# Edge biases summed in 64 buckets of one tile and 16 columns instead of 32 buckets of two tiles and 32 columns, in one kernel of two graph transformer layers

## The reference, cut to what matters

```python
x = x + _L0_gnn_ref(xn, ..., edge_index, edge_attr_16, Wq, bq, Wk, bk, Wv, bv, Wo, bo, We, be, 32) \
      + _L0_mix_ref(xn[None], Wq, Wk, Wv, Wo, bo, proj)      # random feature attention
x = x + _L0_ffn_ref(...)                                     # gated delta rule, 4 experts
x = x + _L1_gnn_ref(xn, edge_attr_64, edge_index, ...) + _L1_mix_ref(xn, ...)
x = x + _L1_ffn_ref(...)
```

## Time and profile before

| | |
|---|---|
| median of 3 runs | 3136.3 us (3127.96 to 3140.72) |
| the profiled execution | 3123.57 us, span 3120.5 us |
| busy, share of the span | PE 91%, DVE 54%, POOL 48%, ACT 40% |
| mean granted TensorE clock | 0.963 of full speed |
| sort on DVE | 39.4 to 137.2 us from the span's start |
| random feature stage after the sort | 180.4 to 646 us |
| bias stage, first to last add | 655.4 to 819.4 us |

### The profile page before, as it was taken

The page is one execution under the profiler, slowest core; times in us unless marked ns, Lnnn a source line. Parts: engine busy times, 40 slices in busy tenths (PEclk is TensorE's granted clock), DMA queues, the critical chain, the costliest instruction groups (busy, mean ns, idle before and its releaser), DMA issues.

```text
span 3120.5 us, 46071 instructions
## 1 busy us (share of the span) xinstructions
PE 2838.8 (91%) x16072; PEld 1657.1 (53%) x16072; DVE 1674.4 (54%) x3673; ACT 1245.0 (40%) x2883; POOL 1503.9 (48%) x1469
## 2 busy tenths in 40 slices
PE   6999999988899989968999998999989999999828
PEld 3433466667677644446777765444534444444324
DVE  7633355568544452256777743442258989521361
ACT  3312432269322222255666542221057888431201
POOL 0565756568754438643333203554667777200004
PEclk9999999999999999979999998999999999999859
DMA  5400001120111134524445555211167777400504
GB/s 178 144 20 5 7 23 42 55 73 18 28 48 48 46 115 164 199 81 133 132 130 147 149 157 159 84 54 50 31 193 234 227 224 216 138 15 12 189 0 136
DMA packets 275656, 320.31 MB, mean 103 GB/s; under 512 B 155759, under 2 KB 193521, under 8 KB 275428
## 3 DMA queue, kind: packets, MB, share of 16 engines
q1 hardware_dynamic: 219540, 182.05, 19.2%
q0 software_dynamic: 51680, 134.08, 14.0%
q10 hardware_dynamic: 4208, 1.25, 0.2%
HBM read 214.70 MB, written 104.60 MB: 102 GB/s over the span
## 4 chain that ended last, share of the span: by engine, by line
PE 69%; POOL 8%; issue 7%; ACT 6%; DVE 6%; DMA 2%; SPq 1%; ACTq 0%; PEld 0%; DVEq 0%; POOLq 0%; PEldq 0%
POOL conv_src L2757 7%; PE bank L1534 5%; PE bank L714 4%; PE bank L2420 4%; PE bank L1312 4%; PE bank L2984 4%; PE bank L2977 4%; PE bank L445 3%; PE bank L737 2%; PE bank L768 2%; PE bank L1123 2%; PE bank L2400 2%; PE bank L1322 2%; PE bank L864 2%; PE bank L2177 2%
## 5 line engine op out<-in xcount | busy, mean ns | idle before, releaser
L2757 POOL DMA_INDIRECT conv_src<-xn_rows,keep x286 | 291.1, 1018 | 110.3 <-issue 91.6
L297 POOL DMA_INDIRECT sorted_bias<-perf_rec,place x256 | 259.3, 1013 | 146.3 <-PE bank L714 91.9
L2862 DVE TENSOR_TENSOR conv_msg<-bank,conv_src 128x1024 f32<-128x1024 f32 x143 | 175.1, 1224 | 52.8 <-PE bank L2777 40.5
L672 POOL DMA_INDIRECT sorted_edge<-rec,place x128 | 126.8, 991 | 128.7 <-PE bank L1373 69.1
L1953 POOL TENSOR_TENSOR delta_dec<-delta_dec,rates_of 128x512 f32<-128x512 f32 x64 | 67.4, 1053 | 227.4 <-ACT delta_dec L2012 227.4
L1123 PE MATMUL bank<-bias_prod,bias_hot 128*128 128x256 f32 x640 | 148.3, 387 | 25.3 <-ACT bias_hot L1076 13.1
L2777 PE MATMUL bank<-conv_we,conv_eT 64*128 64x512 f32 x572 | 164.2, 651 | 0.2 <-ACT conv_eT L2834 0.2
L1107 POOL TENSOR_TENSOR bias_prod<-bias_col,bias_rec 128x512 f32<-128x512 f32 x128 | 147.3, 1181 | 16.5 <-PE bank L1123 15.7
L1123 PEld LDWEIGHTS bank<-bias_prod,bias_hot 128*128 128x128 f32 x640 | 120.1, 192 | 53.9 <-issue 28.2
L2786 PE MATMUL bank<-conv_msg,conv_hot 128*128 128x512 f32 x288 | 143.5, 621 | 0.0
L2219 DVE TENSOR_TENSOR delta_BA<-bank,delta_dec 128x512 f32<-128x512 f32 x128 | 82.1, 683 | 97.3 <-issue 59.8
(11 more groups left out here) (510 smaller groups left out, 6996.6 us busy)
## 6 DMA issues: line engine op xcount, KB each, us to landing
keep<-slot_qkv SPq DMA_DIRECT2D x32, 512.0 KB, 4.8
delta_kv<-slot_qkv SPq DMA_DIRECT2D x32, 512.0 KB, 3.9
sorted_edge<-sort_pad SPq DMA_DIRECT2D x8, 1440.0 KB, 7.0
keep<-sorted_edge SPq DMA_DIRECT2D x18, 640.0 KB, 4.5
slot_out<-delta_o SPq DMA_DIRECT2D x64, 128.0 KB, 2.7
conv_src<-xn_rows,keep POOLq DMA_INDIRECT x286, 3.8
X<-in_x SPq DMA_DIRECT2D x4, 1024.0 KB, 11.3
sorted_bias<-perf_rec,place POOLq DMA_INDIRECT x256
```

The costliest lines, as they stand in the source:

```text
L297: POOL.indirect_dma_start(out=sorted_bias, out_offset=bass.IndirectOffsetOnAxis(ap=place[:, 0, c:c + 1], axis=0), in_=rec0[:, c, :], in_of ...
L672: POOL.indirect_dma_start(out=sorted_edge, out_offset=bass.IndirectOffsetOnAxis(ap=place_[:, c - skip:c - skip + 1], axis=0), in_=rec1[:, ...
L2757: POOL.indirect_dma_start(out=src[:, n % 4, j, :], out_offset=None, in_=xn_rows, in_offset=bass.IndirectOffsetOnAxis(ap=rec[:, g % 3, k + ...
L2862: DVE.tensor_tensor(msg[:, q, :, :], pairs[1 + q][:, :, :], src[:, n % 4, :, :], ALU.add).then_inc(*raw.up())
```

## The change

- `PARTS = 4` in place of `HALVES = 2`: 64 buckets of 16 columns. `TB = 1`: a bucket is filled up to one tile, so there are again `256 + 16*4*1 = 320` tiles. `W = H * GW` falls from 256 to 128 columns.
- The sort for the biases takes four steps, with that for the edges five; `ranks_after = (4, 10, 16, 22, 29)`. The reduction L553 becomes four additions of 2048, 1024, 512 and 256 elements. The scaling of `prj` moves ahead of the last step. `starts(0)` moves behind the blanking transfers on SP. `offset` becomes the last of the passed signals. `last` lies in another buffer.
- In the bias stage PE makes one product of 128 columns for each tile, each into a bank of its own, and DVE adds each: 320 adds of 128 columns, each with its wait for the last one. POOL makes all 160 multiplications, now of 128 x 256. ACT makes `hot` for four blocks of five, DVE for the fifth with one comparison of 128 x 512. DVE picks five blocks ahead, and the picks are 4 x 16 wide.
- In the attention stage the bias is read in runs of 16.

```diff
-HALVES = 2
-GW = G // HALVES
+PARTS = 4
+GW = G // PARTS
+TB = 1
 TG = 2
-EB = EC + NT * HALVES * TG
+EB = EC + NT * PARTS * TB
...
-            starts(0)
             for i in (5, 6, 7):
                 blanks(i - 2)
                 attributes(i)
             blanks(6)
             blanks(7)
+            starts(0)
...
-            ranks_after = (4, 11, 18)
+            ranks_after = (4, 10, 16, 22, 29)
...
-            size = TG * P
+            size = (TB if n < NT * PARTS // NK else TG) * P
...
-            step(DVE.tensor_reduce(to, run.rearrange("p b c -> p c b"), AX.X, ALU.add))
+            for k in (8, 4, 2):
+                step(DVE.tensor_tensor(run[:, 0:k, :], run[:, 0:k, :], run[:, k:2 * k, :], ALU.add))
+            step(DVE.tensor_tensor(to, run[:, 0, :], run[:, 1, :], ALU.add))
...
-            ranks_of(1, 1, pos[:, 1, :])
-            step(DVE.tensor_tensor(pos[:, 0, :], pos[:, 0, :], pos[:, 1, :], ALU.add))
-            places_of(0, NT * HALVES, H * GW)
+            for part in range(1, NT * PARTS // NK):
+                ranks_of(part, part, pos[:, 1, :])
+                step(DVE.tensor_tensor(pos[:, 0, :], pos[:, 0, :], pos[:, 1, :], ALU.add))
+            places_of(0, NT * PARTS, H * GW)
+            DVE.wait_ge(*prj_in.at(32))
+            DVE.tensor_scalar(prj[:, :], prj[:, :], -dn, None, ALU.mult).then_inc(*scaled.up())
...
-            DVE.wait_ge(*prj_in.at(32))
-            DVE.tensor_scalar(prj[:, :], prj[:, :], -dn, None, ALU.mult).then_inc(*scaled.up())
...
-        passed = [x for x in early_signals + ... + [c_in] if x.total]
+        passed = [x for x in early_signals + ... + [c_in] if x.total and x is not offset]
+        passed += [offset]
...
+            AHEAD = 5
+            def on_vector(b):
+                return b % 5 == 4
...
             def pool():
...
+                for i in range(0, EB, 2):
...
+                    g, k, q = i // PER, i % PER, i % 8
+                    POOL.wait_ge(*picked.at(i // SOME + 1))
+                    if i >= 8:
+                        POOL.wait_ge(*summed.at(i - 6))
+                    POOL.tensor_tensor(prod[:, q:q + 2, :, :], ...).then_inc(*multiplied.up())
...
             def tensor():
+                for i in range(EB):
+                    if i % SOME == 0:
+                        PE.wait_ge(*hot_ready(i // SOME))
+                    if i % 2 == 0:
+                        PE.wait_ge(*multiplied.at(i // 2 + 1))
+                    if i >= 8:
+                        PE.wait_ge(*added.at(i - 7))
+                    PE.matmul(bank[i % 8][:, 0:W], hot[:, i // PER % 2, i % PER, :],
+                              prod[:, i % 8, :, :].rearrange("p h j -> p (h j)"), start=True, stop=True).then_inc(*summed.up())
...
             def vector():
+                def make_hot(b):
...
+                    DVE.tensor_tensor(hot[:, g % 2, ks, :], rep(const("iota"), SOME), mid(rec[:, g % 3, ks, H], P),
+                                      ALU.is_equal).then_inc(*by_dve.up())
...
-                for b in range(3):
+                for b in range(AHEAD):
                     pick(b)
+                    if on_vector(b):
+                        make_hot(b)
...
-                for u in range(groups):
+                for u in range(EB):
...
-                    if by_vector(u + 2) and u + 2 < groups:
-                        multiply(DVE, u + 2, by_dve)
                     DVE.wait_ge(*summed.at(u + 1))
                     if u >= 1:
                         DVE.wait_ge(*added.at(u))
                     DVE.tensor_tensor(flat[:, bass.ds(at, W)], flat[:, bass.ds(at, W)], bank[u % 8][:, 0:W],
                                       ALU.add).then_inc(*added.up())
-                    if u % 2 == 0 and u // 2 + 3 < blocks:
-                        pick(u // 2 + 3)
+                    b = u // 4 + AHEAD
+                    if u % 4 == 0 and b < blocks:
+                        pick(b)
+                    if u % 4 == 2 and b < blocks and on_vector(b):
+                        make_hot(b)
```

More of the change, by code:

```diff
@@ L271, in program @@
         ints = sb("ints", [P, 2, NK], I32)
-        last = sb("last", [P, NT * HALVES])
-        above = sb("above", [P, 3, NT * HALVES])
+        last = va2[:, 2 * NK * EC:2 * NK * EC + NT * PARTS]
+        above = sb("above", [P, 3, NT * PARTS])
         starts_at = sb("starts_at", [P, 2, 3])
@@ L600, in vector @@
             DVE.tensor_copy(extra[:, :, 1].bitcast(I32), src)
-            step(DVE.tensor_single_scalar(tmp[:, :], dst, GW, ALU.bitwise_and))
+            step(DVE.tensor_single_scalar(tmp[:, :], dst, G - GW, ALU.bitwise_and))
             step(DVE.tensor_copy(pos[:, 1, :], tmp[:, :]))
@@ L703, in pool @@
             scatter_edges(rec1, 0, EARLY_CHUNKS, sc_edge, attr_in, extra_in, ahead)
-        passed = [x for x in early_signals + of_norm + [half_set] + ea_in + small_in + x_in + [c_in] if x.total]
+        passed = [x for x in early_signals + of_norm + [half_set] + ea_in + small_in + x_in + [c_in] if x.total and x is not offset]
+        passed += [offset]
         assert len(passed) <= 3 * NT
@@ L1030, in program @@
         biased = ExitStack()
-        bias = biased.enter_context(nc.sbuf_tensor("bias", [P, NT, HALVES, H, GW], F32))
+        bias = biased.enter_context(nc.sbuf_tensor("bias", [P, NT, PARTS, H, GW], F32))
         wq, wk = two_w
@@ L1045, in program, with vectors, hot_ready @@
             far = sb("far", [P, 2, SOME, P])
-            cleared, rec1_set, apart, prepared, picked, by_pool, by_dve, summed, added = signals = sig.several(9)
+            cleared, rec1_set, apart, by_act, by_dve, picked, multiplied, summed, added = signals = sig.several(9)
             rec_in = sig.several(3, "hw")
-            blocks, groups = EB // SOME, EB // TG
-            def by_vector(u):
-                return u % 5 == 4
+            blocks = EB // SOME
+            AHEAD = 5
+            def on_vector(b):
+                return b % 5 == 4
+            def vectors(b):
+                return sum(on_vector(x) for x in range(b))
+            def hot_ready(b):
+                return by_dve.at(vectors(b) + 1) if on_vector(b) else by_act.at(b - vectors(b) + 1)
             def sync():
@@ L1069, in scalar, with near @@
             def scalar():
-                def near(b):
+                mine = [b for b in range(blocks) if not on_vector(b)]
+                def near(n):
+                    b = mine[n]
                     g, ks = tiles_of(b)
-                    ACT.wait_ge(*apart.at(b + 1))
+                    ACT.wait_ge(*apart.at(n + 1))
                     if b * SOME >= 2 * PER:
-                        ACT.wait_ge(*summed.at((b * SOME - 2 * PER + SOME) // TG))
-                    ACT.activation(hot[:, g % 2, ks, :], far[:, b % 2, :, :], AF.Relu, bias=1.0, scale=-1.0
-                                   ).then_inc(*prepared.up())
@@ L1079, in scalar @@
-                for b in range(blocks):
+                        ACT.wait_ge(*summed.at(b * SOME - 2 * PER + SOME))
+                    ACT.activation(hot[:, g % 2, ks, :], far[:, n % 2, :, :], AF.Relu, bias=1.0, scale=-1.0
+                                   ).then_inc(*by_act.up())
+                for n, b in enumerate(mine):
                     g, ks = tiles_of(b)
                     ACT.wait_ge(*rec_in[g % 3].at(16 * (g // 3 + 1)))
-                    if b >= 2:
-                        ACT.wait_ge(*prepared.at(b - 1))
+                    if n >= 2:
+                        ACT.wait_ge(*by_act.at(n - 1))
@@ L1143, in vector @@
                             bucket[0:1, 0, u:u + 4], engines=(mybir.EngineType.DVE,), min_val=0,
-                            max_val=(NT * HALVES - 1) * W, skip_runtime_bounds_check_because="the sort has bounded them")
+                            max_val=(NT * PARTS - 1) * W, skip_runtime_bounds_check_because="the sort has bounded them")
                     at = starts[u % 4]
-                    if by_vector(u + 2) and u + 2 < groups:
-                        multiply(DVE, u + 2, by_dve)
                     DVE.wait_ge(*summed.at(u + 1))
```

58 lines of the change are left out of this document (20 added, 38 removed).

## The result

The changed kernel takes 3142.1 us in the median of six runs (3136.9 to 3147.6), the kernel before 3134.5 in six beside them (3124.3 to 3140.7). The ratio is **1.0037, 95% interval 1.0021 to 1.0054**: 11.6 us or 0.4% more. That is "same" by the prediction's bound of 0.5%, though the upper end of the interval passes it a little. The two medians by themselves lie 7.6 us apart. Forecast were 3149 us and 13.1 us more. The profiled execution took 3140.3 us.

The account below looks back on a forecast made before the run. The prediction took DVE's adds, multiplications and waiting picks to set the bias stage's pace, with POOL as busy, and PE to pace the sort. Terms 6.3 + 1.1 + 1.0 + 4.7 = 13.1 us gave 3149 us; 8-in-10 range 3138 to 3174.

Parts of the forecast that it names:

- The sort, 4.7 us: End of the sort: DVE free at 186.5 us, after PE's first scores would be due, moving the score stage 4.7 us later.
- The stage, 6.3 us: Bias stage: DVE's 320 adds, 80 loads and 16 comparisons take 170.3 us against 164.0, so 6.3 us more.
- The start, 1.1 us: Start of the bias stage: five picks and a comparison on DVE ahead of its memset, 1.1 us before the first add.
- The clock, 1 us: After the bias stage: PE's granted clock may fall, so the next stage starts slowly; 1 us, 0 to 4.
- PE near half busy: Bias stage: a sign to be seen after the change, PE's busy share in the stage near half.
- The first record load: Start of the bias stage: a sign to be seen, the first record load 4 to 6 us later than before.
- The scatter is hidden: POOL's scatter transfers: start later, 49 us late at first, caught up before the bias stage, so they cost nothing.
- What bounds the stage before: Old bias stage: twenty tiles cost 10.4 us, a sum of DVE's adds, multiplications and waiting picks; ACT and PE rarely last.
- Picks meet POOL: Rival, bias stage: DVE's picks wait for POOL's multiplications, 12 us if half meet, 43 if all; total 3174; chance 0.25.
- The wait is free: Rival, bias stage: waiting for the last add costs nothing, stage about 40 us shorter, total 3103; chance 0.06.
- The sort stays hidden: Rival, end of the sort: its 4.7 us becomes 1, total +5 with adds at 0.47, 3141 us; chance 0.12.
- POOL does not catch up: Rival, scatter: transfers lose time and the bias stage starts 10 to 20 us late, total 3165; chance 0.05.

Follow-up runs that it names:

- sort alone: The changed sort feeding the bias stage of the kernel before, against the kernel before: ratio 1.0022 (1.0007 to 1.0037), +6.9 us.
- run 3: The changed kernel with all 80 comparisons of 128 x 512 left to ACT, none on DVE: ratio 1.0036 (1.0018 to 1.0054) to the kernel before.
- run 4: The changed kernel without accumulation, each add's result put into one of eight buffers, so adds don't wait for one another: ratio 0.9891 to the kernel before.
- run 5: The kernel before without accumulation, its 160 adds put into a ring of eight buffers, none waiting for the last: ratio 1.0004 (0.9981 to 1.0026).
- run 12: The changed kernel with each pick behind the second add of its block of four instead of the first: ratio 1.0143 to the kernel before.
- runs 4 and 6: run 4, and the changed kernel with even and odd tiles added into two tables, joined at the end: ratio 0.9947 to the kernel before.
- run 9: The changed kernel with the reduction in place of the four additions in all five sort steps: ratio 1.0061 (1.0039 to 1.0083) to the kernel before.
- run 7: The changed kernel with rank sums of four of five sort steps issued inside feature products, last pair in product 28: ratio 1.0039 to the kernel before.
- run 10: The changed kernel with rank sums of four sort steps inside feature products, last pair in product 29 instead of 28: ratio 1.0105 to the kernel before.

## Why the prediction was right, point by point

The size and the class came out as forecast, +11.6 for +13.1 us. That the sum is so close is in part luck. By the trace the stages up to the end of the bias stage make 12.8 us, of which the sort has 3.1 us more than its term (the later start is 1.3 of it, the cost of PE's standstill 2.0, and the sort itself took 0.2 less) and the three other terms together 3.4 us less. The terms:

- **The sort, 4.7 us.** Measured 5.7 at the first reduction, some 1.3 of it a later start that PE shows already near 41 us (a row at 42.09 against 40.84), so the sum of the steps (end at 186.5) was good to half a microsecond, and the additions take 4.7 us as forecast. Mis-sized is what the delay becomes: PE's standstill of 5.11 us is followed by 2.0 us more at the lower clock, so 7.7 us (sort alone: +6.9 in time). The prediction had put a clock term at the bias stage and none here.
- **The stage, 6.3 us.** Measured 4.8. Spacing of adds 0.488 (forecast 0.485), a load 0.09 (0.11), picks next to nothing: right. The comparisons were mis-sized, 0.23 us each in place and 0.16 by run 3, for 0.41: loads and comparisons share one gap, and the sum counted each as if it stood alone.
- **The start, 1.1 us**: measured 0.2. The five picks take 0.77 us together.
- **The clock, 1 us**: the granted clock is 0.99 over the stage, and the trace shows no such cost beyond the spread of what follows.
- **PE near half busy** was one of the signs, and did not come (83%). The price of the products was right (run 4); what was missed is that the profile's busy time of PE grows where its products are held up.
- **The first record load** was to come 4 to 6 us later, and comes 7.8 later (654.70 against 646.94): the sort's delay again.
- **The scatter is hidden**: transfer 240 of 256 is 7.7 us late, just as PE is, so POOL had caught up. It waits for PE again from transfer 219 on, at 456.5 us and not by 450 as forecast. Right where it was forecast, and the step to distrust elsewhere: the argument asked who waits for the transfers, not what runs beside them, and where before takes 3214 us the stage beside them grows by 42 us.
- **What bounds the stage before** was read wrongly. The sum of DVE's ten adds, two multiplications and waiting picks gave 10.1 of 10.4 us for twenty tiles, and yet without the wait the adds gain nothing (run 5). A gap of 0.20 us behind a named wait was real but not last: something in the loop of POOL, PE and ACT was. The change moves the bound from that loop to DVE's chain, and the two happen to be equally long. That the two are equally long was not reasoned out, and is luck as far as the prediction goes. The forecast came out because DVE's new chain was worked out from rows, and was set against the measured 164 us and not against a model of it.

The rivals. *Picks meet POOL*: tried in run 12, where they take 0.41 us instead of 0.23; even then 2.9 us, so its price (12 us where half of the picks meet) was four times too high. *The wait is free*: refuted by runs 4 and 6. Its adds would have followed at 0.29 us; without the wait they follow at 0.20, with it at 0.49. The Trainium skill (VectorE: DVE Perf Modes, "The DRAIN you can't avoid") has it that "the semaphore costs nothing extra here"; in this kernel it costs 0.29 us between two adds. That an operation which isn't held starts earlier, as the same section adds, agrees with run 4. *The sort stays hidden*: refuted by 187.5 us and run 9. *POOL does not catch up*: it does.

## What to carry to other kernels

- An operation that waits for its forerunner costs its own time, the gap and the overlap that it forgoes: here 0.49 instead of 0.20 us. Narrower pieces only multiply that. Two tables with a join at the end (41 us won, 12 paid) won more than any of the trims tried here.
- To find what bounds a loop of four nearly full engines, take one wait away; the sum of one engine's work can come out right for the wrong engine. Here DVE's sum was 10.1 of 10.4 us, and its wait was worth nothing.
- A transfer that is moved needs two questions: who waits for it, and what runs beside it. And work on an engine that has slack is free only to the point where it is ready last; past that it costs one to one, plus what the standstill costs PE in clock.

## What the runs showed that had not been expected

- Adds of 128 x 128 overlap: starts 0.20 us apart at 0.28 us each.
- A standstill of PE costs more than itself: one of 5.0 us was followed by 4.1 us at the lower clock, 2.0 us lost (run 7), one of 5.1 us behind the sort by 2.0 us more as well (the changed kernel).
- Executions differ by up to 2.3 us already at the sort's first running sum (42.37 to 44.69 us), so delays are best counted from a common point: the first reduction of kernels with the same sort lies between 186.0 and 188.1 us, and between 143.54 and 143.58 from the first running sum.
- The same kernel takes 3127, 3128 and 3134.5 us in three sets of runs and 3214 on a chip of its own. The change costs 0.4% where it was measured, beside 3134.5 us, and by the estimates above 1.1% to 1.3% where the kernel before takes 3214.

No version here is shown to beat the kernel before everywhere: two tables do by 0.5% to 0.7% where it takes 3128 us, and, with the sums of run 10, not where it takes 3214. Those sums with two tables were not run on the first.
